# The causal triangle in the small score tiles of the maxima: added by VectorE instead of multiplied in by TensorE

## What is computed

```
xn = layernorm(x)
q, k, v = xn Wq^T, xn Wk^T, xn Wv^T         # 16 heads of 16
s = softmax(causal(rope(q) rope(k)^T / 4)) v  Wo^T
g = silu(ffn(xn))                            # gated feed-forward part, 1024 wide, with Hadamard transforms
out = x + s * g
```

## Time and profile before

| | |
|---|---|
| median of 3 runs | 836.98 us (836.44, 836.98, 840.16) |
| the profiled execution | 834.53 us, span of its instructions 832.8 us |
| busy | TensorE 786.3 us (94%), VectorE 561.9 (67%), ScalarE 498.4 (60%), GpSimd 419.3 (50%) |
| granted TensorE clock, mean | 0.995 |
| chain that ended last | TensorE 56%, VectorE 8%, GpSimd 3%, ScalarE 2% |

### The profile page before, as it was taken

One profiled execution on the slowest core, in us unless ns is written; L12 is line 12 of the kernel. 1 busy time (PEld: TensorE's weight loads), 2 busy tenths in 40 slices (PEclk: granted clock), 3 DMA queues, 4 the chain that ended last, 5 costly groups with the idle time before them and its releaser, 6 DMA issues.

```text
span 832.8 us, 14495 instructions
## 1 busy us (share of the span) xinstructions
PE 786.3 (94%) x5212; PEld 479.8 (58%) x5212; DVE 561.9 (67%) x1017; ACT 498.4 (60%) x684; POOL 419.3 (50%) x476
## 2 busy tenths in 40 slices
PE   3999999999988999999999999999999999999997
PEld 2678888888755554554545454554444554555444
DVE  3785555445467777777776767777777677777635
ACT  2455475453543667657676666676766567676561
POOL 4569758475571464322655434265372135737343
PEclk9999999999999999999999999999999999999998
DMA  9143452453541222333333352335434242443321
GB/s 319 50 152 127 152 171 81 145 162 126 190 92 52 65 64 60 95 90 117 91 117 115 105 165 90 91 105 127 125 95 141 77 118 92 126 131 114 137 73 52
DMA packets 61055, 95.71 MB, mean 115 GB/s; under 512 B 10360, under 2 KB 27448, under 8 KB 60984
## 3 DMA queue, kind: packets, MB, share of 16 engines
q1 hardware_dynamic: 59400, 92.94, 36.9%
q10 hardware_dynamic: 1584, 1.84, 0.7%
HBM read 57.54 MB, written 36.95 MB: 113 GB/s over the span
## 4 chain that ended last, share of the span: by engine, by line
PE 56%; DVE 8%; POOL 3%; ACT 2%; issue 2%; DMA 2%; SPq 0%; DVEq 0%; POOLq 0%; ACTq 0%
PE ps L1369 14%; PE ps L335 11%; PE ps L1347 10%; PE ps L1324 9%; PE ps L345 6%; DVE ps L1623 4%; PE ps L1410 3%; DVE mx L1628 2%; PE ps L1335 1%; ACT a_sb L355 1%; DVE a_sb L376 1%; POOL a_sb L390 1%; ACT probs L1512 1%; DMA scr_heads<-o_raw 1%; DMA late<-scr_inv 1%
## 5 line engine op out<-in xcount | busy, mean ns | idle before, releaser
L1512 ACT ACTIVATE probs<-ps 128x1024 f32<-128x1024 f32 (+1 forms) x320 | 292.5, 937 | 110.0 <-PE ps L1347 108.5
L1628 DVE TENSOR_REDUCE mx<-ps 128x4 f32<-128x512 f32 (+1 forms) x192 | 215.6, 1134 | 85.5 <-PE ps L1324 51.5
L1207 POOL TENSOR_SCALAR_AFFINE_SELECT probs<-probs 128x256 f32<-128x256 f32 (+1 forms) x192 | 92.7, 487 | 259.7 <-ACT probs L1512 258.9
L1623 DVE CUSTOM_DVE_ANT_0 ps<-ps,tri 128x384 f32<-128x384 f32 (+1 forms) x256 | 154.6, 647 | 25.2 <-PE ps L1324 25.0
L1369 PE MATMUL ps<-probs,v_ones 128*32 128x512 f32 (+3 forms) x1584 | 158.6, 490 | 3.6 <-POOL probs L1207 3.1
L1347 PE MATMUL ps<-q_s,k_s 64*128 64x512 f32 (+3 forms) x768 | 143.6, 400 | 10.3 <-DVE mx L1623 4.5
L1324 PE MATMUL ps<-k_s,q_s 48*128 48x512 f32 (+3 forms) x768 | 137.3, 383 | 6.1 <-DVE mx L1623 2.5
L1347 PEld LDWEIGHTS ps<-q_s,k_s 64*128 64x128 f32 x768 | 68.9, 186 | 107.7 <-issue 79.4
L1324 PEld LDWEIGHTS ps<-k_s,q_s 48*128 48x128 f32 x768 | 69.7, 185 | 74.2 <-ACT probs L1512 51.4
L390 POOL TENSOR_TENSOR a_sb<-a_sb,u_sb 128x512 f32<-128x512 f32 x64 | 83.2, 1307 | 57.0 <-ACT u_sb L363 31.2
L335 PE MATMUL ps<-xh,wug_hi 128*128 128x512 f32 x256 | 106.4, 415 | 3.7 <-DVE rot L858 1.9
(11 more groups left out here) (145 smaller groups left out, 1051.7 us busy)
## 6 DMA issues: line engine op xcount, KB each, us to landing
scr_qk<-kinds SPq DMA_DIRECT2D x64, 256.0 KB, 2.4
q_s<-scr_qk SPq DMA_DIRECT2D x64, 128.0 KB, 2.8
k_s<-scr_qk SPq DMA_DIRECT2D x64, 128.0 KB, 3.0
scr_heads<-o_raw SPq DMA_DIRECT2D x30, 256.0 KB, 2.1
x_sb<-in_x SPq DMA_DIRECT2D x8, 512.0 KB, 5.5
scr_v<-v_st SPq DMA_DIRECT2D x16, 256.0 KB, 2.9
q_s<-scr_qk SPq DMA_DIRECT2D x64, 64.0 KB, 2.9
k_s<-scr_qk SPq DMA_DIRECT2D x64, 64.0 KB, 3.0
```

Source lines behind the costliest of these rows:

```text
L1207: pool.affine_select(out=part, in_=part, compare_op=ALU.is_ge, fill=0.0, base=0, pattern=pattern, channel_multiplier=-1).then_inc(cut, 1)
L1512: act.activation(probs[:, n % 2, p, :, 0:w], ps[:, bank:bank + 2, 0:w], ACT.Exp, scale=SCALE).then_inc(exp_ok, 1)
L1623: last = dve.tensor_tensor_reduce(part_of, part_of, sh.tri[:, CH - w:CH], 1.0, LOWEST, ALU.add, ALU.max, mx[:, v % 2, kind, h, i % TPC:i % ...
L1628: last = dve.tensor_reduce(out[:, :, pairs[0]:pairs[0] + n], ps[:, banks[0]:banks[0] + 2, 0:n * w].rearrange('p e (x k) -> p e x k', x=n), ...
```

## The change

`max_tile` no longer issues the four mask products; the last score product of a small tile counts up `tile_ok`. `read_tile` adds, for a small tile, a VectorE instruction ahead of the reduction: it adds the triangle to the last 128 columns of each of the four heads, in place in PSUM, and counts up a new semaphore, `masked`, on which VectorE itself waits before it reduces. `MASKED_TO[k]` is the number of small tiles among the first k + 1. The bf16 constants are still made.

```diff
@@ -43,6 +43,7 @@
         w = min(P * (i + 1) - CH * part, CH)
         TILES += [(i, part, w, (0, 1))] if 2 * w <= CH else [(i, part, w, (0,)), (i, part, w, (1,))]
 NT = len(TILES)
+MASKED_TO = [sum(len(t[3]) == 2 for t in TILES[:k + 1]) for k in range(NT)]
 LOW_TILES = sum(i < TPC for i, _, _, _ in TILES)
 
 
@@ -995,6 +996,7 @@
 
         ones_set, wo_in, wo_high, wo_ok = (sem('ones1_set'), sem('wo_in'), sem('wo_high'), sem('wo_ok'))
         row_in = [[sem(f'row_in{c}{i}') for i in range(2)] for c in range(QC)]
+        masked = sem('masked')
         tile_ok, tile_read, high_ok, mt_ok, shift_ok = (
             sem('tile_ok'), sem('tile_read'), sem('high_ok'), sem('mt_ok'), sem('shift_ok'))
         scored, exp_ok, cut, pv_ok, o_taken = (
@@ -1317,22 +1319,12 @@
                 if k in (0, LOW_TILES):
                     pe.wait_ge(sh.qk_in[v % 2][int(k > 0)], 16 * QK_LOADS * (v // 2 + 1))
                 wait_banks(('tile', v, k))
-                masked = len(pairs) == 2
                 for n, p in enumerate(pairs):
                     for e in range(2):
                         rows = slice(SLOT * e, SLOT * e + ROWS)
                         last = pe.matmul(ps[:, banks[e], n * w:(n + 1) * w],
                                          q[rows, i // TPC, p, i % TPC * P:(i % TPC + 1) * P],
-                                         keys[rows, part, p, 0:w], start=n == 0, stop=not masked)
-                if masked:
-
-                    for late in range(2):
-                        for e in range(2):
-                            rows = slice(SLOT * e, SLOT * (e + 1))
-                            cols = slice(SLOT * (e + 1 - late), SLOT * (e + 1 - late) + P)
-                            out = ps[:, banks[e], 0:2 * w].rearrange('p (x k) -> p x k', x=2)[:, :, w - P:w]
-                            rhs = sh.mask[rows, cols].rearrange('p (one k) -> p one k', one=1).to_broadcast([SLOT, 2, P])
-                            last = pe.matmul(out, sh.one_hot[rows, cols], rhs, start=False, stop=late == 1)
+                                         keys[rows, part, p, 0:w], start=n == 0, stop=n == len(pairs) - 1)
                 last.then_inc(tile_ok, 1)
 
             def scores(u, s, p):
@@ -1625,9 +1617,14 @@
                 else:
                     n = len(pairs)
                     out = mx[:, v % 2, kind, :, i % TPC].rearrange('p (e x) -> p e x', e=2)
-                    last = dve.tensor_reduce(out[:, :, pairs[0]:pairs[0] + n],
-                                             ps[:, banks[0]:banks[0] + 2, 0:n * w].rearrange('p e (x k) -> p e x k', x=n),
-                                             axis=AX.X, op=ALU.max)
+                    of_heads = ps[:, banks[0]:banks[0] + 2, 0:n * w].rearrange('p e (x k) -> p e x k', x=n)
+                    if n == 2:
+
+                        ahead = of_heads[:, :, :, w - P:w]
+                        tri = sh.tri[:, CH - P:CH].rearrange('p (a b k) -> p a b k', a=1, b=1).to_broadcast([P, 2, n, P])
+                        dve.tensor_tensor(ahead, ahead, tri, op=ALU.add).then_inc(masked, 1)
+                        dve.wait_ge(masked, MASKED_TO[k] + MASKED_TO[-1] * v)
+                    last = dve.tensor_reduce(out[:, :, pairs[0]:pairs[0] + n], of_heads, axis=AX.X, op=ALU.max)
                 last.then_inc(tile_read, 1)
                 if k == NT - 1:
                     dve.wait_ge(tile_read, nth_tile(v, k) + 1)
```

## The result

The changed kernel takes 854.82 us (median of 4 runs, 851.19 to 856.21) against 836.71: 18.1 us more, a ratio of 1.0196 with a 95% interval of 1.0169 to 1.0223. Forecast were 851 and a range of 839 to 863. A second set gave 853.75 and 1.0185 [1.0159, 1.021]. The profiled execution took 853.73 us, with a span of 852.0, which is 19.2 more than the 832.8 before. Part of the 19.2 is the clock: the mean granted clock of TensorE was 0.995 in the profiled execution of the kernel before and is 0.985 here.

A forecast was written before the change was run, and what follows sets the result against it. Bound: TensorE's order together with PSUM hand-overs waiting for VectorE's readings. Terms 8.6 + 3.4 + 1.5 + 1.3 = 14.8 us, less 2 gives 12.8; on 834.53 that is 849.0, plus 2.45 for the median 851.5, said 851; range 839 to 863.

The forecast's parts named there:

- The mechanism: Banks 4 and 5 pass on without slack; add and wait end a reading 0.72 us later, 0.48 if VectorE was idle.
- Tile 11: Banks 4 and 5, next round's second scores: no slack in 15 units, nine at 0.48 and six at 0.72, 8.6 us.
- Tile 1 with tile 3 close behind: Banks 0 and 1, seven units: tile 3 waits for tile 2's reading with 0.05 us slack, 7 x 0.48 = 3.4 us.
- Tile 1 with tile 3 further off: Seven other units: the transpose of the maxima in bank 0 waits instead, 0.24 us each, 1.5 us in all.
- Unit 1: First unit beside attention: VectorE comes from splitting output weights and reads tiles 1 and 2 back to back, about 1.3 us.
- Tiles 0 and 8: Banks 2 and 3: slack of 0.5 to 1.4 us just holds the 0.48 delay, the saved 0.24 is not won; 0.
- Unit 0: No attention beside it: three masks saved (0.7 us) against one wait of tile 11 for tile 9 (0.7); 0.
- Recovered elsewhere: TensorE's waits for GpSimd, 3.1 us in two places, do not move with the delay and take 2 us back.
- The clock: Rival: gathered stalls in rounds 4 and 0 make TensorE's clock fall, 1.7 us each; most units 24 us, 875; 13%.
- the rival's price: Rival that the saved products win: TensorE keeps 0.24 us in some 46 tiles, -11 us, 826 us; 7%.
- VectorE falling behind: Rival: jobs queue behind longer readings, tiles 0 and 8 cost 0.25 us each too, 7 us more, 858 us; 8%.
- the clock falling in half of the units: Smaller form of the rival that stalls make TensorE's clock fall: 863 us, the range's upper end; 13% for the rival.

The follow-up runs named there:

- e4: Against the changed kernel: VectorE adds the triangle for tiles 1 and 11 only, TensorE masks tiles 0 and 8 by products again; 853.40 us, ratio 1.0189.
- e6: Against the changed kernel: VectorE adds the triangle for tile 1 only, TensorE masks the other three small tiles by products again; 840.20 us, ratio 1.0042.
- e1: Against the kernel before: the 256 mask products removed with nothing in their place, maxima of small tiles running over masked scores too; 833.24 us, ratio 0.9961.

## Why the prediction was right

**The mechanism** held: no slack in banks 4 and 5, 0.72 us per add with its wait (measured 0.695 + 0.03), the loss at tiles 1 and 11 and not in VectorE's total. At the same clock the change costs 851.3 - 837.2 = 14.1 us, where the sum had 12.8 without the clock. That the two are so close is in part luck: the terms below miss by up to 2 us each, in both directions.

**Term by term**, measured in the order of time of the changed kernel, in units where the clock did not fall:
- Tile 11, 8.6 predicted: the scores behind it come 0.56 us later in nine units and about 1.0 in six, after 0.23 had been gained. 9 x 0.33 + 6 x 0.73 = 7.3. In the nine I had forgotten that the product came 0.18 us behind its weights; now it starts with them, and some 0.15 us of the delay are swallowed there.
- Tile 1 with tile 3 close behind, 3.4: seven units, 0.50 to 0.57, together 3.6 (in two of them tile 0 has brought half of it forward).
- Tile 1 with tile 3 further off, 1.5: 0.04 to 0.2 in most of the seven, since the transpose waits, but the 0.15 to 0.24 saved ahead of it pays for that. But in unit 11 a transpose of x in bank 0 comes directly behind tile 1, a job order that I had not looked at, and costs 0.5 (the same in e4, where the clock did not fall there). All seven together give 1.3.
- Unit 1, 1.3: 3.7 in the profile, together with 7 us at a clock of 0.51. Tile 1 alone cost 0.45 there in e6, where the clock did not fall.
- Tiles 0 and 8, 0: 0.28 in three units (counted above, two with the near and one with the far ones) and 0.74 in unit 1 at tile 0; tile 8 nothing (in the units where TensorE gained 0.13 it gave it back at tile 9). The price of 0.48 was wrong at tile 0: VectorE came to it without a pause in ten of 15 units, so 0.72 to 0.77 applies; mostly the slack held even that. And the slack was not 0.5 to 1.4 us in all units: in unit 1 it was 0.05.
- Unit 0, 0: 0.5 lost; what the masks of tiles 0 and 1 had given is gone again by tile 8, and tile 11 waits 0.6 longer.
- Recovered elsewhere, -2: not seen; TensorE waits 3.8 us for GpSimd in two places, where it had been 3.1.

With unit 1 taken from the runs without a fall (0.74 + 0.45) the terms give 7.3 + 3.6 + 1.3 + 1.2 + 0.5 = 13.9, close to the 14.1 at the same clock.

**The clock**, one more fall or 1.7 us, was under-sized: 0.9896 to 0.9857 is 0.0039, at 0.5 to 0.8 us per 0.001 2 to 3 us. The profiled execution of the kernel before, from which I counted one fall in the main loop, had a clock of 0.995, as high as the best of its 54 executions, and their mean is 0.9896: it was no typical one. And I put the cause in the stalls alone, while the runs tie it at least as much to the work removed.

**Wrong** was the rival's price: that TensorE, with the add hidden, would keep 0.24 us in 46 tiles. e1 takes the add away altogether and keeps a third. I had read "no wait for VectorE in front of the next product" as "this product bounds the kernel"; it was followed, further on, by another wait that does not move. The rivals of VectorE falling behind and of the clock falling in half of the units did not come about. The reduction behind an add starts 0.03 us after its end, never 0.08 before, so the wait had its price. The Trainium skill (VectorE: DVE Perf Modes, The DRAIN you can't avoid) says that such a semaphore costs nothing extra; the traces of this case do not bear that out.

## What to carry to other kernels

Work moved from an engine that is 94% busy to one that is 67% busy can lose, when the second holds PSUM banks meanwhile: price it as a longer hold, at each hand-over where the next user loads its weights within 0.05 us of the release, and expect only the places without slack to count. Before the order of products is changed to gain slack, look at what the moved product itself waits for. And products that are taken away give back only what no later wait takes: here a third.

## What the hardware did that I had not expected

- TensorE's granted clock fell more often in kernels with fewer small bf16 products (0.9855 to 0.9878 against 0.989 to 0.992), some 2 to 3 us in this change, with the cause open. In the profiled executions it falls at nearly the same places of the program in different kernels: units 0, 1, 6, 11 and 12, and the end.
- Executions of one kernel differ by 8.8 us (832.65 to 841.46), nine tenths of the variance with the mean clock, so a change of 0.5% is told apart only beside the clock.
